# A batch's carry as an identity matmul into PSUM, one register load per batch, full-width clears

## The chip, the cores and the metric

One core of a Trainium2 chip. The time is device microseconds (us) of the whole program. The median of three runs of the kernel before is 1608.08 us (1603.89 to 1608.5).

## The reference

A three-layer graph step over 3125 nodes of 256 features with 50000 weighted edges (dst sorted, src not), and then a mixture of 16 experts, top 2. What matters here is the graph step, whose sparse matrix the kernel first builds as a dense one, for use in all three layers:

```
def _spmm(vals, row, col, h, n_nodes):
    msgs = vals[:, None] * h[col]
    return segment_sum(msgs, row, num_segments=n_nodes)
for _ in range(LAYERS):
    h = _l2_normalize(_spmm(vals, row, col, h, n_nodes));  acc = acc + h
x = x + acc / (LAYERS + 1)
```

In the program's call row is src and col is dst, and the edge list is sorted by dst. The output is x after that and after the expert layer.

## The kernel before

The program runs six phases one after another: phase_tables, phase_build, phase_rounds, phase_route, phase_experts, phase_combine. The change touches the first two; a barrier of all engines stands between phases.

phase_tables turns the sorted edge list into tables. Edges lie in tiles of 128. A step pairs one tile with one window of destination nodes (CW nodes, whose HI x LO rows of sources fill 120 x 160 numbers); tile and window advance like a staircase, so that there are 912 steps (STEPS), in 76 batches (NB) of 12 (B, BATCH). The tables hold for each step the marks of its edges (marks: key, low part of the source, the weight in three bf16 parts) and its place in PSUM (place: a slot of 160 columns, three slots to a bank of 512, four banks), and for each batch the window it starts at (base) and the slot of the batch before in which its first window lies (slot, by line 288). same says whether two batches share an edge tile's step at their border.

phase_build makes the dense matrix a_rows in DRAM. Per batch b:

- VectorE (one_hots, weigh, lines 465 to 480) compares tables with marks: key_hot (line 470), lo_hot (472), and three weighted copies key_w (479), the third only for half of the steps. It starts batch b when batch b - 2 is multiplied (two buffers, u).
- ScalarE (third, line 424) makes the other six third weights (433), and evacuates the four banks of PSUM into win, a ring of four batches (evacuate, 436, line 444).
- TensorE (multiply, 541) waits for the evacuation of batch b - 2, loads registers with the places of two batches in every even batch (24 registers, line 547), clears four banks with matmuls on zeros that are 2 columns wide (552, start=True), waits for hot_ready and third_ready, and adds 12 x 3 matmuls of 128 x 160 (558) at the places in the registers.
- VectorE adds the carry of batch b - 2 (carry, 496, line 504): the slot of the batch before it, in which a window was left unfinished, times same_b, onto its first slot in win. The slots are registers, four loaded per four batches (slots_of, 488, line 491); same_b is copied out by line 486.
- SP (store, 400) loads base (401), waits for carried, and stores the batch's window rows in four DMAs, one for each 32 partitions (406); each waits for the same part of the batch before.

Batches are unrolled at both ends and loop by four in between (batches, 383, and Fori at 522). phase_rounds reads a_rows after the barrier.

Of the kernel before, what the change touches and what calls it, by code (L numbers as in the profile page):

```python
# [21 lines left out]
I32 = mybir.dt.int32  # L22
U32 = mybir.dt.uint32
ALU = mybir.AluOpType
# [65 lines left out]
def phase_tables(nc, s, x, src, dst, ew, hf, tab):  # L90
    with ExitStack() as ctx:
# [124 lines left out]
        def _(dve):  # L216
# [41 lines left out]
            link(v.tensor_tensor(win_of[:], step_id[:], tile_of[:], ALU.subtract))  # L258
            first = tile_of[:].rearrange("p (b j) -> p b j", j=B)
            v.memset(tab.same[:, 0:1], 0.0)  # L260
            v.tensor_tensor(tab.same[:, 1:s.NB], first[:, 1:s.NB, 0], first[:, 0:s.NB - 1, B - 1], ALU.subtract)

# [24 lines left out]
            link(v.tensor_tensor(moved[:, 1:s.NB], base[:, 1:s.NB], base[:, 0:s.NB - 1], ALU.subtract))  # L287
            link(v.tensor_scalar(moved[:], moved[:], float(B - 1), float(s.LO), ALU.min, ALU.mult))
            v.tensor_copy(tab.slot[:], moved[:])
            v.tensor_scalar(tab.base[:], base, float(s.W - 1), None, ALU.min)  # L290
# [4 lines left out]
            link(v.scalar_tensor_tensor(bank[:], slot[:], float(s.LO), bank[:], ALU.mult, ALU.add))  # L295
            link(v.tensor_copy(tab.place[:], bank[:]))

# [33 lines left out]
def phase_build(nc, s, tab, a_dram):  # L331


    with ExitStack() as ctx:
# [16 lines left out]
        zeros = sb("zeros", [P, s.HI * LO])  # L351
        same_b = sb("same_b", [P, 2])
        third_b = sb("third_b", [P, 2, B])
        none = sb("none", [P, 512], BF16)
        win = sb("win", [P, RING, B * LO])
        ps_w = ctx.enter_context(nc.psum_tensor("ps_w", [P, 2, BANKS * 512], F32))

        tabs = sem("tabs")
        same_read = sem("same_read")
        third_read = sem("third_read")  # L360
# [4 lines left out]
        evacuated = sem("evacuated")  # L365
        carried = sem("carried")
        padded = sem("padded")
# [25 lines left out]
        @block.sync  # L393
        def _(sp):
            first = s.W * CW
            sp.wait_ge(tabs, 3)
            sp.dma_start(a_dram.rearrange("i (c n) l -> (i c) (n l)", c=CW)[first:s.CH * P, :],
                         zeros[0:s.CH * P - first, :]).then_inc(padded, 16)

            def store(b, i):  # L400
                base = sp.value_load(tab.base[0:1, one(b)], min_val=0, max_val=s.W - 1)
                sp.wait_ge(carried, b + 1)
                for n, part in enumerate(PARTS):
                    if late(b, 1):
                        sp.wait_ge(stored[n], b * 16)
                    sp.dma_start(a_dram[bass.DynSlice(base, B), part, :].rearrange("i p l -> p i l"),
                                 win[part, i, :].rearrange("p (i l) -> p i l", l=LO)).then_inc(stored[n], 16)

            sp.wait_ge(padded, 16)
            for b in range(NB):  # L410
                store(b, b % RING)
            for done in stored:
                sp.wait_ge(done, 16 * NB)

        @block.gpsimd
        def _(pool):
            g = nc.gpsimd
            g.memset(none[:], 0.0).then_inc(tabs, 1)
            g.memset(zeros[:], 0.0).then_inc(tabs, 1)
            g.memset(win[:, RING - 1, :], 0.0).then_inc(tabs, 1)  # L420

        @block.scalar
        def _(act):
# [12 lines left out]
            def evacuate(b, i):  # L436
                if late(b, RING):
                    act.wait_ge(carried, b - 2)
                    for done in stored:
                        act.wait_ge(done, (b - 3) * 16)  # L440
                act.wait_ge(tabs, 3)
                act.wait_ge(multiplied, b + 1)
                for bank in range(BANKS):
                    ins = nc.scalar.activation(win[:, i, bank * WIDE:(bank + 1) * WIDE],  # L444
                                               ps_w[:, i % 2, bank * 512:bank * 512 + WIDE], ACT.Copy)
                ins.then_inc(evacuated, 1)
# [10 lines left out]
        def _(dve):  # L457
# [23 lines left out]

            def same(b, u):

                if late(b, 2):
                    dve.wait_ge(carried, b - 1)
                v.tensor_copy(same_b[:, u:u + 1], tab.same[:, one(b)]).then_inc(same_read, 1)

            def slots_of(b, n):

                at = slice(b, b + n) if isinstance(b, int) else bass.DynSlice(b, n)  # L490
                _, values = nc.values_load_multi_w_load_instructions(
                    tab.slot[0:1, at], engines=[mybir.EngineType.DVE], min_val=0, max_val=(B - 1) * LO,
                    skip_runtime_bounds_check_because="a slot is LO times the minimum with B - 1 of a count")
                return values

            def carry(b, i, slot):

                there = bass.DynSlice(slot, LO)
                start = slice(0, LO)
                dve.wait_ge(evacuated, b + 1)  # L500
                dve.wait_ge(same_read, b + 1)
                if late(b, 1):
                    dve.wait_ge(carried, b)
                v.scalar_tensor_tensor(win[:, i, start], win[:, (i - 1) % RING, there], same_b[:, i % 2:i % 2 + 1],
                                       win[:, i, start], ALU.mult, ALU.add).then_inc(carried, 1)

            def run(b, i, slot):
                u = i % 2
                one_hots(b, u)
                weigh(b, u, 0)  # L510
                weigh(b, u, 1)
                if late(b, 2):
                    same(b - 2, u)
                weigh(b, u, 2)
                if late(b, 2):
                    carry(b - 2, (i - 2) % RING, slot)

            dve.wait_ge(tabs, 3)
            slots = slots_of(0, 2)
            for b in range(RING):  # L520
                run(b, b, slots[b - 2] if b >= 2 else None)
            with dve.Fori(1, NB // RING) as it:
                slots = slots_of(it * RING - 2, RING)
                for i in range(RING):
                    run(it * RING + i, i, slots[i])
            slots = slots_of(NB - 2, 2)
            for b in (NB - 2, NB - 1):
                same(b, b % 2)
                carry(b, b % RING, slots[b - (NB - 2)])

        @block.tensor
        def _(pe):
            mm = nc.tensor.matmul
            pe.wait_ge(tabs, 3)
            for bank in range(2 * BANKS):
                mm(ps_w[:, bank // BANKS, bank % BANKS * 512:(bank % BANKS + 1) * 512], none[:, 0:P], none[:, :],
                   start=True, stop=True, skip_group_check=True)

            places = []

            def multiply(b, i):
                u = i % 2
                if late(b, 2):
                    pe.wait_ge(evacuated, b - 1)
                if u == 0:
                    both = slice(b * B, (b + 2) * B) if isinstance(b, int) else bass.DynSlice(b * B, 2 * B)
                    places[:] = nc.values_load_multi_w_load_instructions(
                        tab.place[0:1, both], engines=[mybir.EngineType.PE], min_val=0,
                        max_val=(BANKS - 1) * 512 + (PER - 1) * LO,
                        skip_runtime_bounds_check_because="a place is made of a slot below B, whatever the edges are")[1]  # L550
                for bank in range(BANKS):
                    mm(ps_w[:, u, bank * 512:bank * 512 + 2], none[:, 0:P], none[:, 0:2],  # L552
                       start=True, stop=False, skip_group_check=True)
                pe.wait_ge(hot_ready, (b + 1) * 4)
                pe.wait_ge(third_ready, (b + 1) * BY_ACT)
                for j in range(B):
                    for k in range(3):
                        ins = mm(ps_w[:, u, bass.DynSlice(places[u * B + j], LO)], key_w[:, u, k, j // 2, :, j % 2],  # L558
                                 lo_hot[:, u, j // 2, :, j % 2],
                                 start=False, stop=False, skip_group_check=True)  # L560
                ins.then_inc(multiplied, 1)

# [1120 lines left out]
class Tables:  # L1683


    def __init__(self, nc, ctx, s):
# [5 lines left out]
        self.marks = sb("tab_marks", [P, 5, s.STEPS], BF16)  # L1692
        self.same = sb("tab_same", [P, s.NB])
        self.place = sb("tab_place", [1, s.STEPS], I32)
        self.slot = sb("tab_slot", [1, s.NB], I32)
        self.base = sb("tab_base", [1, s.NB], I32)
# [45 lines left out]
```

## Time and profile before

| | us |
|---|---|
| median of 3 runs | 1608.08 (1603.89 to 1608.5) |
| the profiled execution | 1605.87 |
| its span, first to last instruction | 1604.1 |

The page's first part gives for the whole span: TensorE busy 1259.8 us (79%), VectorE 1137.9 (71%), ScalarE 875.4 (55%), GpSimd 209.8 (13%), and a mean granted TensorE clock of 0.878, where 1 is 2.4 GHz and 0.5 is 1.2 GHz. phase_build runs from some 49 to 465 us. Busy time is that of compute instructions; what a sequencer does (register loads, waits) has rows of its own and isn't in it, and the engine's idle time that comes of it is put down to "issue". Names in rows: PE is TensorE, PEld its weight loads, PEldq and DVEq the sequencers of TensorE and VectorE, SPq SP's queue, DVE VectorE, ACT ScalarE, POOL GpSimd.

### The profile page before, as it was taken

The page shows a single profiled execution, that of the slowest core. Times are in us where ns is not written, and L with a number is a line of the kernel's source. Part 1 is how long each engine was busy: PE and PEld are TensorE (multiplying, and loading weights), DVE is VectorE, ACT ScalarE, POOL GpSimd, SP SyncE. Part 2 cuts the span into 40 slices and gives each one's busy share as a digit, 9 for nine tenths or more (in the row PEclk, how much of TensorE's full clock was granted, in tenths as well). Part 3 has the DMA queues.
Part 4 walks back from the last instruction along what each step waited for, and adds up shares of the span by engine and source line. Part 5 has one row for each costly group of instructions (what it writes and reads, how often), then busy time and mean ns, then how long its engine had stood idle before and what let it go on. Part 6 is the DMA issues. An engine that isn't in the chain of part 4 may idle for free. (4 is left out here: it accounts for less than half of the span.)

```text
span 1604.1 us, 31106 instructions
## 1 busy us (share of the span) xinstructions
PE 1259.8 (79%) x9152; PEld 1135.5 (71%) x9153; DVE 1137.9 (71%) x2074; ACT 875.4 (55%) x1933; POOL 209.8 (13%) x199
## 2 busy tenths in 40 slices
PE   4467666667648999999999999999754799999600
PEld 1366666666647888888888888888652699999600
DVE  8788888888837656656555766655567498898557
ACT  2577777777735555655545655555321466666312
POOL 1300000000000000000000000000080434444273
PEclk8788887888879999999999999999955799999955
DMA  3187777677787666656666666666222587334373
GB/s 95 45 206 189 181 178 173 166 173 174 182 235 209 183 187 185 182 166 178 187 194 183 187 166 186 176 195 183 88 95 70 188 269 235 109 103 110 118 232 113
DMA packets 228741, 267.64 MB, mean 167 GB/s; under 512 B 16053, under 2 KB 172348, under 8 KB 228582
## 3 DMA queue, kind: packets, MB, share of 16 engines
q1 hardware_dynamic: 205392, 234.01, 52.5%
q0 software_dynamic: 6624, 16.90, 3.9%
q10 hardware_dynamic: 16640, 15.73, 3.2%
q8 instruction: 36, 0.59, 0.1%
q14 instruction: 49, 0.40, 0.1%
HBM read 175.51 MB, written 91.07 MB: 166 GB/s over the span
## 5 line engine op out<-in xcount | busy, mean ns | idle before, releaser
L865 PE MATMUL ps_rows<-h_both,a_high 128*128 (+1 forms) x1875 | 509.7, 400 | 29.4 <-DVE a_low L745 24.1
L745 DVE TENSOR_TENSOR a_low<-a_raw,a_high 128x640 fp32r<-128x640 f32 x375 | 305.8, 823 | 239.0 <-ACT a_high L675 236.0
L675 ACT ACTIVATE a_high<-a_raw 128x640 fp32r<-128x640 f32 x375 | 274.6, 740 | 297.2 <-PE ps_rows L868 283.5
L865 PEld LDWEIGHTS ps_rows<-h_both,a_high 128*128 128x128 f32 x1875 | 332.7, 192 | 87.7 <-issue 24.5
L868 PEld LDWEIGHTS ps_rows<-h_both,a_low 128*128 128x128 f32 x1875 | 277.4, 191 | 33.2
L868 PE MATMUL ps_rows<-h_both,a_low 128*128 (+1 forms) x1875 | 285.7, 283 | 0.0
L558 PE MATMUL ps_w<-lo_hot,key_w 128*128 128x160 bf16 x2736 | 258.5, 264 | 33.1 <-DVE key_w L479 31.0
L558 PEld LDWEIGHTS ps_w<-lo_hot,key_w 128*128 128x128 bf16 x2736 | 243.4, 112 | 37.7 <-issue 35.9
L444 ACT ACTIVATE win<-ps_w 128x480 f32<-128x480 f32 x304 | 147.3, 567 | 71.5 <-PE ps_w L558 57.6
L479 DVE TENSOR_TENSOR key_w<-key_hot,tab_marks 128x1536 bf16<-128x1536 bf16 (+1 forms) x228 | 178.2, 814 | 0.0
L433 ACT ACTIVATE key_w<-key_hot,third_b 128x128 bf16<-128x128 bf16 x456 | 144.5, 426 | 38.2 <-DVE key_hot L470 36.9
L1353 POOL DMA_INDIRECT x_t<-tokens,r_token x80 | 104.4, 1305 | 131.5 <-PE ps_x L1480 118.7
L1367 ACT ACTIVATE w_high<-w_raw 128x1024 fp32r x80 | 80.4, 1052 | 63.1 <-PE ps_o L1512 53.6
L470 DVE TENSOR_TENSOR key_hot<-key_tab,tab_marks 128x1536 bf16<-128x1536 bf16 x76 | 72.3, 951 | 58.6 <-PE ps_w L558 31.2
L1425 DVE TENSOR_TENSOR w_low<-w_raw,w_high 128x1024 fp32r<-128x1024 f32 x80 | 94.4, 1220 | 17.6 <-ACT w_high L1367 12.9
L1495 PE MATMUL ps_h<-x_high,w_high 128*128 128x256 f32 x320 | 94.8, 296 | 0.0
L1011 POOL MEMSET all_ones<- 128x800 f32 x1 | 0.8, 764 | 699.5 <-POOLq L572 699.5
L1495 PE MATMUL ps_h<-x_low,w_high 128*128 128x256 f32 x320 | 91.4, 286 | 0.0
L1495 PE MATMUL ps_h<-x_high,w_low 128*128 128x256 f32 x320 | 91.4, 286 | 0.0
L1512 PE MATMUL ps_o<-w_high,hid_high 128*128 128x256 f32 x320 | 90.0, 281 | 1.3 <-DVE hid_low L1440 1.3
L552 PE MATMUL ps_w<-none 128*128 128x2 bf16 x304 | 18.9, 166 | 91.3 <-issue 91.3
L1512 PE MATMUL ps_o<-w_low,hid_high 128*128 128x256 f32 x320 | 90.1, 281 | 0.0
(225 smaller groups left out, 1576.0 us busy)
## 6 DMA issues: line engine op xcount, KB each, us to landing
a_raw<-a_rows SPq DMA_DIRECT2D x375, 320.0 KB, 3.1
a_rows<-win SPq DMA_DIRECT2D x228, 240.0 KB, 3.6
w_raw<-in_L_ffn_w SPq DMA_DIRECT2D x32, 512.0 KB, 5.0
a_rows<-win SPq DMA_DIRECT2D x76, 180.0 KB
results_sorted<-y_t ACTq DMA_DIRECT2D x40, 256.0 KB, 3.2
b_t<-in_L_ffn_b ACTq DMA_DIRECT2D x40, 128.0 KB, 3.6
hf<-in_x SPq DMA_DIRECT2D x1, 3072.0 KB
x<-in_x SPq DMA_DIRECT2D x1, 3072.0 KB
```

The lines of the kernel that those rows point to most:

```text
L433: nc.scalar.activation(key_w[:, u, 2, j // 2, :, j % 2], key_hot[:, u, j // 2, :, j % 2], ACT.Copy, scale=third_b[:, u, j:j + 1]).then_inc ...
L444: ins = nc.scalar.activation(win[:, i, bank * WIDE:(bank + 1) * WIDE], ps_w[:, i % 2, bank * 512:bank * 512 + WIDE], ACT.Copy)
L479: v.tensor_tensor(key_w[:, u, k, 0:n, :, :], key_hot[:, u, 0:n, :, :], mark(b, 2 + k, P)[:, 0:n, :, :], ALU.mult).then_inc(hot_ready, 1)
L558: ins = mm(ps_w[:, u, bass.DynSlice(places[u * B + j], LO)], key_w[:, u, k, j // 2, :, j % 2], lo_hot[:, u, j // 2, :, j % 2], start=False ...
L675: a.activation(a_high[:, u, :], a_raw[:, u, :], ACT.Copy).then_inc(high_split, 1)
L745: v.tensor_tensor(a_low[:, u, :], a_raw[:, u, :], a_high[:, u, :].bitcast(F32), ALU.subtract).then_inc(low_split, 1)
L865: nc.tensor.matmul(ps[:, banks[w][r], :], a_high[:, u, r * P:(r + 1) * P], both, start=first, stop=False, skip_group_check=True)
L868: ins = nc.tensor.matmul(ps[:, banks[w][r], 0:D], a_low[:, u, r * P:(r + 1) * P], upper, start=False, stop=last, skip_group_check=True)
L1353: g.indirect_dma_start(out=x_t[:, t % 2, h, :], out_offset=None, in_=y_dram, in_offset=bass.IndirectOffsetOnAxis(ap=routes.token[:, t * HA ...
L1425: v.tensor_tensor(w_low[n][:, u, :], of_expert(w_raw[n], e), w_high[n][:, u, :].bitcast(F32), ALU.subtract).then_inc(w_low_ready[n], 1)
L1495: ins = mm(ps_h[:, u, f, :], w[0][:, u, at], x[:, u, k, :], start=(n == 0), stop=(n == 3 * KD - 1))
L1512: ins = mm(ps_o[:, u, half, :], h[:, u, f, tokens], w[1][:, u, at], start=(n == 0), stop=(n == 3 * KF - 1))
```

## The change

The carry moves from VectorE to TensorE. After a batch's 36 matmuls TensorE waits for the evacuation of the batch before (evacuated, b) and multiplies the identity (fp32, made by GpSimd) with the 160 columns of win that hold the slot, into the batch's first place. same, same_b, the semaphores same_read and carried, and tab.slot are gone; whether there is a carry is now told by the slot alone: it is limited to B instead of B - 1, and win has a thirteenth slot of zeros. tab.place holds 13 numbers per batch, twelve places and the slot, and TensorE loads them in one load per batch, behind the clears. The clears are 512 columns wide, and the eight full clears at the start of the phase are gone. SP waits for evacuated. VectorE's loop has no register load. The waits on tabs move: VectorE and ScalarE have none, TensorE waits for 5.

```diff
-            link(v.tensor_scalar(moved[:], moved[:], float(B - 1), float(s.LO), ALU.min, ALU.mult))
-            v.tensor_copy(tab.slot[:], moved[:])
+            link(v.tensor_scalar(moved[:], moved[:], float(B), float(s.LO), ALU.min, ALU.mult))
+            v.tensor_copy(tab.place[:, :, B], moved[:])
...
-            link(v.tensor_copy(tab.place[:], bank[:]))
+            link(v.tensor_copy(tab.place[:, :, 0:B], bank[:].rearrange("p (b j) -> p b j", j=B)))
...
-        win = sb("win", [P, RING, B * LO])
+        win = sb("win", [P, RING, (B + 1) * LO])
...
-                sp.wait_ge(carried, b + 1)
+                sp.wait_ge(evacuated, b + 1)
...
-            g.memset(win[:, RING - 1, :], 0.0).then_inc(tabs, 1)
+            g.memset(win[:, :, B * LO:(B + 1) * LO], 0.0).then_inc(tabs, 1)
+            g.memset(ones[:], 1.0).then_inc(tabs, 1)
+            pool.wait_ge(tabs, 4)
+            g.affine_select(out=ident[:], in_=ones[:], pattern=[[1, P]], compare_op=ALU.is_equal,
+                            fill=0.0, base=0, channel_multiplier=-1).then_inc(tabs, 1)
...
                 if late(b, RING):
-                    act.wait_ge(carried, b - 2)
                     for done in stored:
                         act.wait_ge(done, (b - 3) * 16)
-                act.wait_ge(tabs, 3)
                 act.wait_ge(multiplied, b + 1)
...
-                v.scalar_tensor_tensor(win[:, i, start], win[:, (i - 1) % RING, there], same_b[:, i % 2:i % 2 + 1],
-                                       win[:, i, start], ALU.mult, ALU.add).then_inc(carried, 1)
...
+            def run(b, i):
                 u = i % 2
                 one_hots(b, u)
...
+                for k in range(3):
+                    weigh(b, u, k)
+
+            batches(dve, run)
...
-            pe.wait_ge(tabs, 3)
-            for bank in range(2 * BANKS):
-                mm(ps_w[:, bank // BANKS, bank % BANKS * 512:(bank % BANKS + 1) * 512], none[:, 0:P], none[:, :],
-                   start=True, stop=True, skip_group_check=True)
...
+            pe.wait_ge(tabs, 5)
...
                 if late(b, 2):
                     pe.wait_ge(evacuated, b - 1)
-                if u == 0:
-                    both = slice(b * B, (b + 2) * B) if isinstance(b, int) else bass.DynSlice(b * B, 2 * B)
-                    places[:] = nc.values_load_multi_w_load_instructions(
-                        tab.place[0:1, both], engines=[mybir.EngineType.PE], min_val=0,
...
                 for bank in range(BANKS):
-                    mm(ps_w[:, u, bank * 512:bank * 512 + 2], none[:, 0:P], none[:, 0:2],
+                    mm(ps_w[:, u, bank * 512:(bank + 1) * 512], none[:, 0:P], none[:, :],
                        start=True, stop=False, skip_group_check=True)
+                values = nc.values_load_multi_w_load_instructions(
+                    tab.place[0:1, one(b), :].rearrange("p b j -> p (b j)"), engines=[mybir.EngineType.PE], min_val=0,
+                    max_val=B * LO,
...
                 pe.wait_ge(hot_ready, (b + 1) * 4)
                 pe.wait_ge(third_ready, (b + 1) * BY_ACT)
...
+                if late(b, 1):
+                    pe.wait_ge(evacuated, b)
+                    ins = mm(ps_w[:, u, bass.DynSlice(places[0], LO)], ident[:, :],
+                             win[:, (i - 1) % RING, bass.DynSlice(slot, LO)],
+                             start=False, stop=False, skip_group_check=True)
                 ins.then_inc(multiplied, 1)
...
-        self.place = sb("tab_place", [1, s.STEPS], I32)
-        self.slot = sb("tab_slot", [1, s.NB], I32)
+        self.place = sb("tab_place", [1, s.NB, s.BATCH + 1], I32)
```

## Rows read from the trace of the kernel before

**Rows 1.** Windows view, all engines: us, busy and count, clock, DMA share, GB/s

```profile
60.00:465.00 405.00, 268.18 (x3031) 257.04 (x3028) 339.47 (x527) 291.98 (x828) 0.00 (x0) 0.83 0.73 175
```

**Rows 2.** Groups by line, 80 to 440: busy us, mean ns, then idle before

```profile
L479 DVE TENSOR_TENSOR key_w<-key_hot,tab_marks 128x1536 bf16<-128x1536 bf16 (+1 forms) x207 | 161.9, 814 | 0.0
L444 ACT ACTIVATE win<-ps_w 128x480 f32<-128x480 f32 x276 | 133.7, 566 | 68.3 <-PE ps_w L558 55.4 <-DMA a_rows<-win 12.9
L433 ACT ACTIVATE key_w<-key_hot,third_b 128x128 bf16<-128x128 bf16 x413 | 131.0, 426 | 25.8 <-DVE key_hot L470 24.6
```

**Rows 3.** Waits, 80 to 440: who waited for what, us in total, times, longest

```profile
PE ps_w L552 <- issue: 88.3, 34, 4.2
DVE key_hot L470 <- issue: 17.3, 7, 3.1
```

**Rows 4.** Single lines, several stretches: count, ns min/median/max, first and last start

```profile
L547 PEldq TENSOR_LOAD <-tab_place x2: 1622/1627/1632, 65.1 to 73.8; - x2
...
L491 DVEq TENSOR_LOAD <-tab_slot x1: 986/986/986, 72.1 to 72.1; - x1
...
L547 PEldq TENSOR_LOAD <-tab_place x34: 1952/3346/4654, 84.1 to 431.8; - x34
...
L491 DVEq TENSOR_LOAD <-tab_slot x17: 1700/2315/3541, 91.5 to 427.6; - x17
...
L547 PEldq TENSOR_LOAD <-tab_place x1: 3797/3797/3797, 293.9 to 293.9; - x1
...
L558 PEldq FUSED_REGOPS  x9: 37/37/42, 297.9 to 298.9; - x9
```

**Rows 5.** Timeline of TensorE: start us, us, what, [idle before <- released by]

```profile
291.98 2.75 PE L558 MATMUL ps_w<-lo_hot,key_w 128*128 128x160 bf16 x36 [0.25 <-DVE key_w L479]
297.72 0.25 PE L552 MATMUL ps_w<-none 128*128 128x2 bf16 x4 [2.99 <-issue]
298.03 4.02 PE L558 MATMUL ps_w<-lo_hot,key_w 128*128 128x160 bf16 x36
...
308.70 4.98 PE L558 MATMUL ps_w<-lo_hot,key_w 128*128 128x160 bf16 x36 [0.91 <-DVE key_w L479]
```

**Rows 6.** Timeline of VectorE around one batch

```profile
291.13 0.14 DVE L486 COPY same_b<-tab_same 128x1 f32 x1
291.19 0.55 DVE L479 TENSOR_TENSOR key_w<-key_hot,tab_marks 128x768 bf16<-128x768 bf16 x1
291.65 0.38 DVE L504 SCALAR_TENSOR_TENSOR win<-win,same_b 128x160 f32<-128x160 f32 x1
291.95 0.95 DVE L470 TENSOR_TENSOR key_hot<-key_tab,tab_marks 128x1536 bf16<-128x1536 bf16 x1
...
296.45 0.95 DVE L470 TENSOR_TENSOR key_hot<-key_tab,tab_marks 128x1536 bf16<-128x1536 bf16 x1
```

**Rows 7.** Timeline at the phase's two ends

```profile
54.27 3.60 PE L536 MATMUL ps_w<-none 128*128 128x512 bf16 x8 [16.32 <-POOL win L420]
...
55.08 0.96 DVE L470 TENSOR_TENSOR key_hot<-key_tab,tab_marks 128x1536 bf16<-128x1536 bf16 x1 [9.13 <-POOL win L420]
...
59.45 2.75 PE L558 MATMUL ps_w<-lo_hot,key_w 128*128 128x160 bf16 x36 [1.50 <-DVE key_w L479]
...
448.39 2.74 PE L558 MATMUL ps_w<-lo_hot,key_w 128*128 128x160 bf16 x36
...
465.27 2.27 SPq L643 DMA_DIRECT2D a_raw<-a_rows  x5
```

**Rows 8.** SP: its register load (78 to 138, then all), and the page's DMA issues

```profile
L401 SPq TENSOR_LOAD <-tab_base x14: 479/692/1094, 78.5 to 137.4; - x14
...
L401 SPq TENSOR_LOAD <-tab_base x76: 467/728/1170, 74.3 to 456.8; - x76
...
a_rows<-win SPq DMA_DIRECT2D x228, 240.0 KB, 3.6
```

**Rows 9.** Single line 1182, a matmul in full fp32 of the route phase

```profile
L1182 PEld LDWEIGHTS ps_l<-gw,yT x100: 287/333/337, 1180.6 to 1209.5; 128*128 128x128 f32 x100
```

More of the change, by code:

```diff
@@ L258, in _ @@
             link(v.tensor_tensor(win_of[:], step_id[:], tile_of[:], ALU.subtract))
-            first = tile_of[:].rearrange("p (b j) -> p b j", j=B)
-            v.memset(tab.same[:, 0:1], 0.0)
-            v.tensor_tensor(tab.same[:, 1:s.NB], first[:, 1:s.NB, 0], first[:, 0:s.NB - 1, B - 1], ALU.subtract)
             dve.wait_ge(x_in, 32)
@@ L351, in phase_build @@
         zeros = sb("zeros", [P, s.HI * LO])
-        same_b = sb("same_b", [P, 2])
+        ones = sb("ones_c", [P, P])
+        ident = sb("ident_c", [P, P])
         third_b = sb("third_b", [P, 2, B])
         none = sb("none", [P, 512], BF16)
-        win = sb("win", [P, RING, B * LO])
+        win = sb("win", [P, RING, (B + 1) * LO])
         ps_w = ctx.enter_context(nc.psum_tensor("ps_w", [P, 2, BANKS * 512], F32))
         tabs = sem("tabs")
-        same_read = sem("same_read")
         third_read = sem("third_read")
@@ L365, in phase_build @@
         evacuated = sem("evacuated")
-        carried = sem("carried")
         padded = sem("padded")
@@ L406, in store @@
                     sp.dma_start(a_dram[bass.DynSlice(base, B), part, :].rearrange("i p l -> p i l"),
-                                 win[part, i, :].rearrange("p (i l) -> p i l", l=LO)).then_inc(stored[n], 16)
+                                 win[part, i, 0:B * LO].rearrange("p (i l) -> p i l", l=LO)).then_inc(stored[n], 16)
             sp.wait_ge(padded, 16)
@@ L480, in weigh @@
                                 ALU.mult).then_inc(hot_ready, 1)
[L482 to L503, printed above, removed]
-                v.scalar_tensor_tensor(win[:, i, start], win[:, (i - 1) % RING, there], same_b[:, i % 2:i % 2 + 1],
-                                       win[:, i, start], ALU.mult, ALU.add).then_inc(carried, 1)
-            def run(b, i, slot):
+            def run(b, i):
                 u = i % 2
                 one_hots(b, u)
[L510 to L529, printed above, removed]
+                for k in range(3):
+                    weigh(b, u, k)
+            batches(dve, run)
         @block.tensor
@@ L533, in _ @@
             mm = nc.tensor.matmul
-            pe.wait_ge(tabs, 3)
-            for bank in range(2 * BANKS):
-                mm(ps_w[:, bank // BANKS, bank % BANKS * 512:(bank % BANKS + 1) * 512], none[:, 0:P], none[:, :],
-                   start=True, stop=True, skip_group_check=True)
-            places = []
+            pe.wait_ge(tabs, 5)
             def multiply(b, i):
@@ L544, in multiply @@
                     pe.wait_ge(evacuated, b - 1)
-                if u == 0:
-                    both = slice(b * B, (b + 2) * B) if isinstance(b, int) else bass.DynSlice(b * B, 2 * B)
-                    places[:] = nc.values_load_multi_w_load_instructions(
-                        tab.place[0:1, both], engines=[mybir.EngineType.PE], min_val=0,
-                        max_val=(BANKS - 1) * 512 + (PER - 1) * LO,
-                        skip_runtime_bounds_check_because="a place is made of a slot below B, whatever the edges are")[1]
                 for bank in range(BANKS):
-                    mm(ps_w[:, u, bank * 512:bank * 512 + 2], none[:, 0:P], none[:, 0:2],
+                    mm(ps_w[:, u, bank * 512:(bank + 1) * 512], none[:, 0:P], none[:, :],
                        start=True, stop=False, skip_group_check=True)
+                values = nc.values_load_multi_w_load_instructions(
+                    tab.place[0:1, one(b), :].rearrange("p b j -> p (b j)"), engines=[mybir.EngineType.PE], min_val=0,
+                    max_val=B * LO,
+                    skip_runtime_bounds_check_because="a place is made of a slot up to B, whatever the edges are")[1]
+                places, slot = [nc.s_assert_within(
+                    place, min_val=0, max_val=(BANKS - 1) * 512 + (PER - 1) * LO,
+                    skip_runtime_bounds_check_because="it is the place of a slot below B") for place in values[0:B]], values[B]
                 pe.wait_ge(hot_ready, (b + 1) * 4)
@@ L557, in multiply @@
                     for k in range(3):
-                        ins = mm(ps_w[:, u, bass.DynSlice(places[u * B + j], LO)], key_w[:, u, k, j // 2, :, j % 2],
+                        ins = mm(ps_w[:, u, bass.DynSlice(places[j], LO)], key_w[:, u, k, j // 2, :, j % 2],
                                  lo_hot[:, u, j // 2, :, j % 2],
                                  start=False, stop=False, skip_group_check=True)
+                if late(b, 1):
[3 more added lines that the diff above has]
+                             start=False, stop=False, skip_group_check=True)
                 ins.then_inc(multiplied, 1)
@@ L1692, in __init__ @@
         self.marks = sb("tab_marks", [P, 5, s.STEPS], BF16)
-        self.same = sb("tab_same", [P, s.NB])
-        self.place = sb("tab_place", [1, s.STEPS], I32)
-        self.slot = sb("tab_slot", [1, s.NB], I32)
+        self.place = sb("tab_place", [1, s.NB, s.BATCH + 1], I32)
         self.base = sb("tab_base", [1, s.NB], I32)
```

## The prediction

> **What bounds the kernel now.** I read the windows first, to find the stage of the change: from 60 to 465 us no engine is full, VectorE is busy 339 us of 405, TensorE 268, ScalarE 292, the DMA engines 0.73, and TensorE's mean granted clock is 0.83 [rows 1]. From 465 us on nothing of the change runs. Then the table of groups in the steady part, where the reader is to see what one batch costs each engine [rows 2]: of VectorE 2.35 us (three weights, 161.9 us for 69 batches), to which key_hot, lo_hot, same_b and the carry come; of ScalarE six weights that run overlapped (131.0 / 69 = 1.90) and the evacuation (133.7 / 69 = 1.94); of TensorE 36 matmuls, whose timeline gives 2.75 us at the full clock and 4.98 at the half [rows 5]. Third, the waits [rows 3]: the longest is TensorE before its four clears, 88.3 us, put down to "issue", so to no other engine; VectorE also waits 17.3 us for "issue". Fourth, the sequencers' rows, which are not counted as busy, name these two: a TENSOR_LOAD, which fetches registers from a table in SBUF [rows 4]. TensorE runs one of 24 registers every second batch (median 3.35 us in 80 to 440), VectorE one of 4 every fourth (2.32). The timeline shows what that does: a load begins at 293.9, beside the last matmuls of the batch that ran from 291.98 to 294.73, lasts 3.80, and the clears start at 297.72, after 2.99 us of idle engine [rows 4, 5].
>
> So two chains take turns. VectorE: 4.50 us from key_hot to key_hot (291.95 to 296.45 [rows 6]); four of them and a load of 2.3 give 20.3 per four batches. TensorE: its loads run from 84.1 to 431.8, 33 steps for 33 pairs [rows 4], 10.54 a pair, 5.27 a batch. Over the stage the first matmul is at 59.45 and the last batch's at 448.39 [rows 5, 7]: 388.9 / 75 = 5.19 us a batch.
>
> **Part 1: the carry leaves VectorE.** 0.38 + 0.14 busy; the next key_hot starts 0.30 after the carry does and the weight 0.06 after same_b [rows 6], so the path loses 0.36: 4.50 becomes 4.14. The load of 4 registers goes too (a median of 2.3 us). VectorE then needs 4 x 4.14 = 16.6 per four batches where it needed 20.3. This is worth 0.9 us a batch if VectorE were alone. It is not: TensorE and the stores are late next.
>
> **Part 2: TensorE's register load, the largest term.** Before: 38 loads of 24. After: 76 loads of 13, one in every batch, on the queue that all matmuls pass. Its time isn't in the trace, so it is bounded by its neighbours [rows 4]. While no store runs: 4 registers 0.99, 24 registers 1.63, which gives 1.28 for 13 on a line. While stores run: 4 take 2.32, 24 take 3.35 (up to 4.65). The ratios are 2.3 and 2.1, so the cost is mostly the company of the stores: line 406 has a store in flight 3.6 us after each issue [rows 8]. In the new order the load falls wholly into a store (below), where the load at 293.9 took 3.80, so I take 13 registers at 3.0, between 2.3 (as 4) and 3.8 (as 24).
>
> In sentences apart: the Trainium skill ("Runtime: NRT & Kernel Launch", Instruction fetch mechanics) says that such a load costs about 200 ns a register even in bulk. The rows don't agree, 4 registers taking 2.32 and 24 taking 3.35; by that rule 13 would be an estimated 2.6, the batch 4.8 and the time some 1571.
>
> **TensorE's cycle after.** Its sequencer runs ahead of the array: nine register steps of three matmuls each were issued from 297.9 to 298.9 [rows 4], 0.12 apart, while the array at the half clock took 0.13 per matmul. From a batch's first matmul: 12 x 0.12 = 1.4 to issue all 36; then the carry (its place and slot arithmetic), four clears and the address of the next load, all issue work, 0.45 (an estimate: the 0.33 between a load's end at 297.70 and the first matmul at 298.03 holds four clears and the steps of the waits [rows 4, 5], and a loop's branch comes every fourth time); the load 3.0; and 0.35 to the next first matmul. Sum 5.2 us a batch. The wait on evacuated in front of the carry stands ahead of the next clears and load on the same queue, so it could delay both. It is satisfied in time: the array ends batch b-1 (2.75, clears and carry behind it) 1.65 before batch b's first matmul, the evacuation takes 1.96 + 0.1 and ends 0.4 after it, and the sequencer reaches the wait at 1.5. ScalarE needs 1.90 + 1.94 and a small copy, 4.1 a batch [rows 2], in the same order as before, and VectorE 4.14: both fit in 5.2.
>
> **Part 3: clears over 512 columns and the carry on the array.** Array time, not issue time. A 512-column matmul on zeros starts each 0.43 us at the half clock (8 in 3.60 [rows 7]), so 0.21 at the full one, x4 = 0.85 where 0.24 stood. The carry is a matmul in full fp32: the rows of line 1182 [rows 9] show 100 entries where 50 were written, so two passes, 0.33 us per weight load at the half clock; for 160 columns I take 0.8 in all, bounds 0.3 and 1.3. At the full clock the array holds 2.6 + 0.85 + 0.8 = 4.2 of 5.2, and 1.0 idle lies inside the 3.0 load. So both are hidden by the load; without that cover they would cost 1.4 a batch. Nor should the clock fall: before, it was at the half level after idle of 2.8 to 3.0 us (the batch at 298.03, 4.02 long, follows a gap of 2.99 [rows 5]), and after no gap is over 1.3. I expect 1.0 in the stage, which gives no time back, since issue and load set the cycle.
>
> **Part 4: stores.** SP waits for evacuated instead of carried. A store could go one to two batches sooner, which frees the ring of win earlier; no time on the path. SP's pace is a floor: while it caught up, 14 of its loads ran from 78.5 to 137.4, 13 steps, 4.53 us a batch [rows 8].
>
> **Part 5: the edges.** POOL's memset of win shrinks to a third and ones and ident are added: I take it that tabs is complete at 54.1, about as before (TensorE started at 54.27 [rows 7]). VectorE no longer waits for it (9.13 us of idle before 55.08 [rows 7]) and is ready; TensorE drops the eight full clears (3.6), and its first matmul waits for a load, 54.1 + 2.7 + 0.4 = 57.2, where it was 59.45: -2.2. Batches 0 to 4, with loads of 1.3, run at VectorE's 4.15, 16.6 in all, the other 71 at 5.2: 385.8 instead of 388.9: -3.1; the stores start only at 74.3 [rows 8], a us sooner perhaps since POOL ends sooner, and the ring holds four batches, which gives back some 1.2. At the end the carries of the last two batches and the stores behind them leave 16.9 us from the last batch's first matmul to the next stage at 465.27 [rows 7]; after: 3.5 (array) + 2.1 + 2.3 (four stores issued) + 4.2 (landing) + 0.8 = 12.9: -4.0. The steps that VectorE loses in the tables stage are worth nothing: it stood idle for 9.13 before 55.08.
>
> **Sum.** -2.2 - 3.1 + 1.2 - 4.0 = -8.1 us: span 1604.1 to 1596.0. The profiled execution is 1605.87, 1.8 above its span and 2.2 below the median of 1608.08. I forecast 1600.0 against the median, -0.5%.
>
> **Rivals.**
> 1. The load is short, and the stores bound. If 13 registers cost 2.3 or less, TensorE's cycle is 4.5 and SP's 4.53 rules: 73.3 + 76 x 4.53 + 4.2 (the last landing) = 422 instead of 465.3, 43 us less, 1565. For it: 4 registers took down to 1.70 beside stores, 24 down to 1.95 [rows 4]. Against: the median of the 4 is already 2.32. The floor holds however short the load is. What lies between this case and mine, a load of 2.3 to 2.75 (1567 to 1582), goes with it. The Trainium skill's rule per register (same page and section) ends there.
> 2. The load costs nearly what 24 cost, since it is paid in every batch now. Place: TensorE's queue between the clears and the first matmul; price: 3.5 to 3.8 gives a cycle of 5.7 to 6.0, 71 x 0.5 - 8 = +28 to 71 x 0.8 - 8 = +49, 1636 to 1657. It decides from a load of 3.11, where the time is that of before. For it: 3.35 is the median of 24 with part of them outside the stores, and the twofold number of loads; against: 24 and 4 differ by 1.0 only, so 13 must lie between.
> 3. The array becomes the bound at the half clock: 4.98 + 1.7 (clears) + 0.9 = 7.6 a batch, +170, some 1778. It needs a clock that stays low; against it, an array that is behind has no gaps.
> 4. The change removes VectorE's work but both chains shift alike and the time stays within 0.3%; this is the middle of my own case.
>
> **How the numbers follow.** 0.3% (4.8 us) is about what a measurement of this kernel can tell. One tenth of a us in the cycle is 7 us. My case, a load of 2.75 to 3.25, has 0.46: 1582 to 1618 by itself, faster 0.26, same 0.13, slower 0.07. Rival 1 and what lies towards it: 0.20, all faster. Rival 2: 0.28, slower. Rival 3: 0.05, slower; rival 4 as a case by itself 0.01. So faster 0.46, same 0.14, slower 0.40. The range goes from rival 1's floor to the middle of rival 2 and leaves out rival 3: 1563 to 1642.
>
> **What would show it.** TensorE's TENSOR_LOAD x76 with a median near 3.0 between 80 and 440 (right), 2.3 (rival 1) or 3.5 (rival 2); first matmuls 5.2 apart; the granted clock near 1.0 in the stage (a 0.83 would break part 3); VectorE idle before key_hot in every batch, waiting for TensorE; no wait of the carry for the evacuation. I am wrong if the load waits for the array to drain, which the load at 293.9 didn't (matmuls until 294.73), or if the carry's wait comes late.

## The result, and the profile after

The changed kernel takes 1843.84 us (median of 4 runs, 1839.07 to 1844.89), the kernel before 1608.29 beside it: ratio 1.1466, 95% interval 1.1437 to 1.1495, slower by 235 us. The forecast was 1600.0, slightly faster, with a range of 1563 to 1642: the time is far above the range and above every rival, the slowest of which was 1778.

The profiled execution has a span of 1841.2 us, 237 more than before. Nearly all of it, 232.5, lies ahead of the next stage's start (697.73 where it was 465.27); the stages behind, which the change doesn't touch, are 4.6 longer. The windows of its steady part, after (first) and before (second); columns as in [rows 1]:

```profile
110.00:400.00 290.00, 173.91 (x1438) 148.93 (x1436) 144.51 (x173) 134.02 (x378) 0.00 (x0) 0.78 0.48 112
```

```profile
110.00:400.00 290.00, 199.07 (x2227) 191.09 (x2228) 248.74 (x386) 212.46 (x606) 0.00 (x0) 0.82 0.74 177
```

Every engine does less in the same 290 us, and the DMA engines move 112 GB/s where they moved 177: the pipeline waits for one thing. The stage's two ends, in TensorE's and SP's timeline, answer [rows 7]:

```profile
56.13 4.25 PE L511 MATMUL ps_w<-lo_hot,key_w 128*128 128x160 bf16 x36 [0.56 <-ACT key_w L433]
...
684.10 4.29 PE L511 MATMUL ps_w<-lo_hot,key_w 128*128 128x160 bf16 x36 [6.14 <-issue]
...
697.73 2.27 SPq L601 DMA_DIRECT2D a_raw<-a_rows  x5
```

(684.10 - 56.13) / 75 = 8.37 us a batch, where it was 5.19; 75 x 3.19 = 239, the whole loss. The waits, 80 to 640, answer [rows 3]:

```profile
ACT win L442 <- PE ps_w L516: 301.6, 49, 9.5
DVE key_hot L468 <- PE ps_w L516: 284.3, 36, 9.2
PE ps_w L511 <- issue: 221.9, 46, 7.3
```

VectorE waits for TensorE at 36 places and ScalarE at 49, of some 67 batches in this window. TensorE waits for its own sequencer and, but for 1.9 us, for nothing else; the wait now stands in front of the matmuls (line 511), since the clears go ahead of the load. The loads, one line each, all 76 and then five in a row, answer [rows 4]:

```profile
L500 PEldq TENSOR_LOAD <-tab_place x76: 1100/3310/8982, 53.7 to 675.8; - x76
...
L500 PEldq TENSOR_LOAD <-tab_place x1: 8871/8871/8871, 266.9 to 266.9; - x1
...
L500 PEldq TENSOR_LOAD <-tab_place x1: 1100/1100/1100, 279.4 to 279.4; - x1
...
L500 PEldq TENSOR_LOAD <-tab_place x1: 8094/8094/8094, 284.1 to 284.1; - x1
...
L500 PEldq TENSOR_LOAD <-tab_place x1: 3099/3099/3099, 295.9 to 295.9; - x1
...
L500 PEldq TENSOR_LOAD <-tab_place x1: 8738/8738/8738, 301.2 to 301.2; - x1
```

The same instruction with the same 13 registers takes 1.10, 3.10 or about 8 to 9 us, and the mean of all 76 is 5.16, where I had taken 3.0. The pattern repeats every four batches: 1.1, 8, 3.1, 8. A row of 13 words is 52 bytes, so batch b starts at 52 b, which lies on a 16-byte border for every fourth b.

The timeline of TensorE over two batches, to be read against [rows 5]:

```profile
282.27 2.74 PE L511 MATMUL ps_w<-lo_hot,key_w 128*128 128x160 bf16 x36
284.85 0.47 PE L516 MATMUL ps_w<-win,ident_c 128*128 x2
285.16 1.03 PE L498 MATMUL ps_w<-none 128*128 128x512 bf16 x4
292.56 4.98 PE L511 MATMUL ps_w<-lo_hot,key_w 128*128 128x160 bf16 x36 [6.38 <-issue]
297.34 0.82 PE L516 MATMUL ps_w<-win,ident_c 128*128 x2
297.95 1.23 PE L498 MATMUL ps_w<-none 128*128 128x512 bf16 x4
```

The load that begins at 284.1, 1.8 after the batch's first matmul, ends at 292.2, and the next first matmul is at 292.56: 1.8 + 8.1 + 0.4 = 10.3 is the step from this batch to the next. After 6.38 us of idle the array is at the half clock (4.98 for the 36).

### The profile page after: what moved, and what is told of

It is laid out like the page before. It is cut to its first block and busy times, and to the rows that moved or that the text cites. A ratio compares the mean times of both kernels' runs of the same rounds, so it can differ in the third digit from the quotient of the medians.

```text
span 1841.2 us, 30942 instructions
## 1 busy us (share of the span) xinstructions
PE 1371.9 (75%) x9294; PEld 1203.7 (65%) x9295; DVE 1114.0 (61%) x1920; ACT 879.0 (48%) x1933; POOL 212.1 (12%) x201
## 5 line engine op out<-in xcount | busy, mean ns | idle before, releaser
L511 PE MATMUL ps_w<-lo_hot,key_w 128*128 128x160 bf16 x2736 | 288.6, 281 | 250.7 <-issue 242.1
L511 PEld LDWEIGHTS ps_w<-lo_hot,key_w 128*128 128x128 bf16 x2736 | 271.1, 119 | 284.1 <-issue 280.4
L477 DVE TENSOR_TENSOR key_w<-key_hot,tab_marks 128x1536 bf16<-128x1536 bf16 (+1 forms) x228 | 174.1, 820 | 0.0
L498 PE MATMUL ps_w<-none 128*128 128x512 bf16 x304 | 81.0, 390 | 15.9 <-POOL ident_c L419 15.9
L1470 PE MATMUL ps_o<-w_high,hid_low 128*128 128x256 f32 x320 | 89.9, 281 | 0.0
```

The lines of the kernel that those rows point to most:

```text
L477: v.tensor_tensor(key_w[:, u, k, 0:n, :, :], key_hot[:, u, 0:n, :, :], mark(b, 2 + k, P)[:, 0:n, :, :], ALU.mult).then_inc(hot_ready, 1)
L511: ins = mm(ps_w[:, u, bass.DynSlice(places[j], LO)], key_w[:, u, k, j // 2, :, j % 2], lo_hot[:, u, j // 2, :, j % 2], start=False, stop=F ...
L1470: ins = mm(ps_o[:, u, half, :], h[:, u, f, tokens], w[1][:, u, at], start=(n == 0), stop=(n == 3 * KF - 1))
```

## The experiments

Three theories were formed from those rows. Theory A: a load whose first word lies on a 16-byte border fetches four registers at a time, any other one; each fetch costs some 0.25 us in quiet and over twice that beside a store. Theory B: only the number of loads and the stores beside them matter. Theory C: the fault is a row that crosses a 64-byte border.

**1. The rows padded to 16 words (e1).**

```diff
-        self.place = sb("tab_place", [1, s.NB, s.BATCH + 1], I32)
+        self.place = sb("tab_place", [1, s.NB, 16], I32)
```

with the load of words 0 to 12 of a row.

> The changed kernel with one edit: a batch's 13 registers start every 16 words of the table instead of every 13. Theory A (start address): a load whose first word lies on a 16-byte border fetches four registers at a time, any other one at a time; each fetch is about 0.25 us in quiet and 0.6 beside a store. Every load is then 4 fetches: 1.1 quiet, at most 2.4, where the changed kernel has a mean of 5.2. Cycle 4.5 to 4.7 us a batch (the stores' pace), time 1560 to 1580, ratio to before 0.97 to 0.98. Theory B (company and count): the 8 us loads are slow because there are 76 of them beside stores, wherever the words lie; nothing changes, 1840. Theory C (64-byte border): a row of 52 bytes crosses one in most batches; padded it doesn't, so as A.

Measured: 1600.34 us, ratio to the kernel before beside it 0.9856, interval 0.9819 to 0.9894: 1.4% faster than before and far from the changed kernel, from one number in a table's shape. Loads, windows, and the last batch's first matmul:

```profile
L500 PEldq TENSOR_LOAD <-tab_place x76: 1103/2718/3640, 53.6 to 426.4; - x76
```

```profile
110.00:400.00 290.00, 226.59 (x2409) 183.47 (x2436) 246.38 (x292) 230.74 (x642) 0.00 (x0) 1.00 0.82 191
```

```profile
429.79 2.75 PE L511 MATMUL ps_w<-lo_hot,key_w 128*128 128x160 bf16 x36 [1.24 <-issue]
```

B falls. The gain is smaller than A's numbers had it: beside stores four fetches take 2.72 in the median, not 2.4 at most, and the cycle is 4.98, not 4.5 to 4.7. The same kernel once more, on another chip, beside experiments 9 and 10:

> The padded kernel once more, on the chip of the two others: ratio 0.982 to 0.989, cycle 5.0. Against the kernel before with quads it should be slower by 0.3 us a batch, 20 us, if the identity matmul costs what its removal gave (0.35 us a batch).

Measured: ratio 0.9825, interval 0.9734 to 0.9916, cycle 5.03. The interval is wide because one run took 1566.47 us where two others took 1589.5 and 1589.7; that run has no trace, and why it was shorter stays open.

**2 and 3. The padded rows, the words starting one and two words in (e2, e3).**

```diff
-                    tab.place[0:1, one(b), 0:0 + B + 1].rearrange("p b j -> p (b j)"), ...
+                    tab.place[0:1, one(b), 1:1 + B + 1].rearrange("p b j -> p (b j)"), ...
```

This is e2 against e1, and the words are written one further, too; e3 has 2 in place of 1.

> As the padded table, but the 13 words start one word into each row of 16: no row crosses a 64-byte border, none starts on a 16-byte one. Theory A: 13 fetches in every batch, 3.1 us in quiet and 8.2 beside stores, cycle about 8.9, time 1860 to 1900. Theory B: 1840. Theory C: as the padded table without the shift, 1560 to 1580.

> The 13 words start two words into each row of 16, on an 8-byte border. Theory A as said (only 16-byte borders count): as the shift by one, 3.1 quiet, 8.2 beside stores, 1860 to 1900. If 8 bytes are fetched at a time where they can be: 7 fetches, 1.8 quiet and 4.3, cycle 6.0 to 6.5, time 1650 to 1700. Theory B: 1840. Theory C: 1560 to 1580.

Measured: 1869.53 and 1875.23 us (one run each), within A's 1860 to 1900. Loads of e2, then e3:

```profile
L500 PEldq TENSOR_LOAD <-tab_place x76: 3097/4325/8680, 53.6 to 691.8; - x76
```

```profile
L500 PEldq TENSOR_LOAD <-tab_place x76: 3097/4435/8980, 53.7 to 690.5; - x76
```

No load is under 3.1 any more, and 3.1 and some 8 alternate. A had counted 8.2 for every load and a cycle of 8.9; the cycles are 8.49 and 8.53, so A's kind is borne out and its price per batch was too high. C falls, since no row of e2 crosses a 64-byte border. An 8-byte border helps nothing: e3 is as e2.

**4. The kernel before, its table moved by one word (e4).** The places are written one word later and read there:

```diff
-                    both = ... bass.DynSlice(b * B, 2 * B)
+                    both = ... bass.DynSlice(b * B + 1, 2 * B)
```

> The kernel before with one edit: its table of places starts one word later, so that its loads of 24 leave the 16-byte border. Theory A: 24 fetches instead of 6, 6 us in quiet, 10 to 15 beside stores, where the kernel before has a mean of 3.2; 38 loads, so 38 x 7 to 38 x 11 us more: 1870 to 2030. Theories B and C: nearly no change, 1605 to 1620 (C: one border more in some loads).

Measured: 1868.33 us (one run), at the lower end of A's 1870 to 2030; B and C had nearly no change. None of the other parts of the change is in it, and it is 246 us slower than the kernel before on this chip (1622.46), where the change cost 235. Its loads, 10.2 us in the mean where they were 3.2:

```profile
L547 PEldq TENSOR_LOAD <-tab_place x38: 6839/10350/14166, 54.3 to 685.2; - x38
```

**5. The changed kernel with small stores (e5).** Each store moves one window instead of twelve, and a_rows is filled with zeros behind the last batch (not shown in the cut), so the output is not the reference's and only the build stage is read.

```diff
-                    sp.dma_start(a_dram[bass.DynSlice(base, B), part, :].rearrange("i p l -> p i l"),
-                                 win[part, i, 0:B * LO].rearrange("p (i l) -> p i l", l=LO)).then_inc(stored[n], 16)
+                    sp.dma_start(a_dram[bass.DynSlice(base, 1), part, :].rearrange("i p l -> p i l"),
+                                 win[part, i, 0:LO].rearrange("p (i l) -> p i l", l=LO)).then_inc(stored[n], 16)
```

> The changed kernel, its table as it is, but each store of a batch moves one of its twelve windows, a twelfth of the bytes; behind the last batch the whole of a_rows is filled with zeros in 25 transfers of 1.6 MB (some 215 us of their own), so the output isn't the reference's and the time of the whole says nothing. What is read is the build stage. Theory A (start address times company): loads of every fourth batch 1.1 us, all others 3.1, none of 8; mean 2.6; cycle 4.9 to 5.0, the last batch's first matmul at 425 to 435 instead of 684. If the company of the stores has no part in it: the 8 us loads stay, 684.

Measured: the last batch's first matmul at 427.66, so a cycle of 4.95, with the DMA engines 0.07 busy from 110 to 400, and nine loads in a row:

```profile
L504 PEldq TENSOR_LOAD <-tab_place x9: 1101/3103/3111, 197.0 to 236.6; - x9
```

The 8 us loads are gone, the 3.1 us ones stay. The two causes are so told apart: where the row starts gives 1.1 or 3.1, the stores make 8 of 3.1. The record of all 76 shows the two classes: loads of every fourth batch 1.16 in the mean, all others 3.1.

**6. The padded kernel with narrow clears (e6).** The clears of a batch are 2 columns wide and the eight full clears stand at the start of the stage, as in the kernel before.

> The padded table, but the four clears of a batch are 2 columns wide again, with the eight full ones at the start of the stage (a slot that no matmul wrote then keeps old numbers, which the carry may read). If the wide clears are hidden by the load, as the prediction had it, and the clock stays: the same time as the padded kernel within 0.3%. If the wide clears are what keeps the clock at its full level: granted clock of the stage 0.85 to 0.95 instead of 1.0, cycle 5.1 to 5.3, 8 to 25 us more. If the array counts after all: 10 to 20 us less.

Measured: ratio 0.9976, interval 0.9949 to 1.0004, on another chip than e1.

```profile
110.00:400.00 290.00, 195.85 (x2310) 188.98 (x2310) 231.86 (x276) 217.30 (x607) 0.00 (x0) 0.91 0.77 180
```

The granted clock is 0.91 where it is 1.00 in e1, the cycle 5.21 where it is 4.98 and, in e11, 5.03 ((447.68 - 56.91) / 75, from the first matmuls' starts). The loads are the same (median 2.72 both). So the wide clears are worth having here: they cost array time that the load hides, and with them the array doesn't fall to the half clock in the steady batches. The prediction had counted them as hidden, but not as a gain.

**7. One load for two batches (e7).** The padded table by pairs, 28 registers in every second batch.

> The padded table laid out by pairs of batches (24 places, 2 slots, the slots once more), one load of 28 registers every second batch: 7 fetches of four for two batches where the padded kernel has 8 in two loads. By issue and load alone the cycle is (2 x 2.1 + 4.2) / 2 = 4.2, so the stores' pace of 4.53 sets the end: last batch's first matmul at 395 to 405, 20 to 33 us less than the padded kernel, ratio to before 0.965 to 0.975. Rival: the gap of 2 us in every second batch lets the clock fall, and the slower array gives the gain back: ratio 0.98 to 0.99, clock under 0.95.

Measured: ratio 1.0243, interval 1.0169 to 1.0317: slower than before, where the padded kernel is faster. I had the loads right and the rest wrong.

```profile
L505 PEldq TENSOR_LOAD <-tab_place x38: 1877/4359/5646, 53.6 to 470.4; - x38
...
L505 PEldq TENSOR_LOAD <-tab_place x1: 4592/4592/4592, 256.3 to 256.3; - x1
```

The waits (80 to 380) seem to name ScalarE's weights; the timeline shows that it isn't they:

```profile
PE ps_w L516 <- ACT key_w L435: 69.7, 24, 3.5
```

```profile
254.11 2.74 PE L516 MATMUL ps_w<-lo_hot,key_w 128*128 128x160 bf16 x36
...
255.62 1.90 ACT L435 ACTIVATE key_w<-key_hot,third_b 128x128 bf16<-128x128 bf16 x6
...
259.43 1.90 ACT L435 ACTIVATE key_w<-key_hot,third_b 128x128 bf16<-128x128 bf16 x6
...
261.21 4.17 PE L516 MATMUL ps_w<-lo_hot,key_w 128*128 128x160 bf16 x36 [3.18 <-ACT key_w L435]
```

The matmuls at 261.21 use the weights that were done at 257.5; those of 259.43 are for the batch behind. The load ends at 260.9, and 0.35 later the matmuls start, as in the padded kernel. So the load is what the array waits for. In 29 steady pairs the weights of ScalarE are done 2.9 us or more before a pair's first matmul, VectorE's 2.4 or more, and the first matmul follows the load's end by 0.26 to 0.35 in all of them. The expectation had counted 2.1 of issue for each of the two batches. But the second batch starts only when the array has done the first: 3.76 us later at the full clock, 5.35 at the half (means). Then come 2.0 of issue, 4.4 of load and 0.35. That is 10.5 us a pair at the full clock, where the padded kernel takes twice 4.98, and 12.0 at the half; 14 of the 29 pairs are of the second kind, such as the one at 261.21, behind 3.18 us of idle. One load for two batches saves about 1.1 us of load time a pair, but no load runs beside the first batch's array time any more.

**8. The padded kernel without the carry's matmul (e8).**

> The padded table; the identity matmul of the carry is left out (the wait in front of it stays), so a window that spans two batches loses the part of the first. If the carry costs array time alone it is hidden by the load: issue 0.1 to 0.2 us less a batch, 5 to 15 us in all. If its end is what starts the next chain (the evacuation, then VectorE and ScalarE) and this chain binds: 0.6 to 0.8 us a batch, 40 to 60 us.

Measured: 1564.07 us against 1604.53 of the kernel before (one run): the last first matmul at 403.50, a cycle of 4.63. By the profiled executions the carry costs 0.35 a batch, 26 us, between the two guesses. This isn't settled: it is one run, the padded kernel's ratios put it at 1576 to 1581 on this chip, only 12 to 17 us more, and one run of e11 took 1566.47 with the carry in it. Of the 0.35, 0.14 is issue (the load begins 1.86 after the first matmul with it, 1.72 without), and 0.22 is in the load itself (mean 2.61 and 2.39), for which I have no shown cause; that the load then falls at another time beside the store is only argued. The stage is now at the stores' pace, 4.53 [rows 8]: over the steady batches the cycle is 4.53, and each batch's store is issued 7.6 us behind its evacuation in the mean and doesn't catch up, where in e1 that lag falls to 0.2.

**9 and 10. Two versions of the kernel before, with the carry on VectorE (e9, e10).** e9 moves the table of slots by two words, so that VectorE's load of four starts on a border; e10 has that and, in every batch, wide clears and behind them one load of 12:

```diff
+                places = nc.values_load_multi_w_load_instructions(
+                    tab.place[0:1, steps(b)], engines=[mybir.EngineType.PE], ...
```

> The kernel before with one edit: the table of slots starts two words later, so that VectorE's load of four begins on a 16-byte border. Theory A: one fetch instead of four, 0.3 us in quiet, 0.6 beside stores, where it has a mean of 2.3; VectorE's four batches take 18.6 us instead of 20.3. TensorE's chain of 10.5 us a pair stands beside it, so the gain is at most half of 1.7 per four batches: 0 to 16 us, ratio 0.990 to 1.0. If start addresses didn't matter: load 2.3, ratio 1.0.

> The kernel before (carry on VectorE) with VectorE's slots on the border, one load of 12 registers in every batch (rows of 48 bytes, all on 16-byte borders, 3 fetches) behind clears of 512 columns; no full clears at the start. So two thirds of the change, without the carry's matmul. Theory A: loads 0.85 quiet, 1.8 beside stores; TensorE's cycle 4.1, VectorE's 4.5 + 0.6/4 = 4.65 binds, clock near 1.0; last batch's first matmul at 59 + 75 x 4.7 = 411, ratio 0.975 to 0.985. If a load in every batch is itself the fault: slower than before.

Measured: e9 0.9915 (0.9885 to 0.9944), e10 0.9793 (0.9762 to 0.9825), 1571.8 us, the lowest ratio of the kernels that were run several times. Their loads, VectorE's of e9 and TensorE's of e10:

```profile
L491 DVEq TENSOR_LOAD <-tab_slot x20: 345/902/997, 54.3 to 433.7; - x20
```

```profile
L542 PEldq TENSOR_LOAD <-tab_place x76: 850/2225/2793, 54.3 to 413.3; - x76
```

The first has a median of 0.90 where it was 2.32 [rows 4], and in quiet, at 72.1, it took 0.38 where it was 0.99. This is VectorE's load, so the start address and not the engine made it dear. The second shows that a load in every batch is no fault: twice the loads of before, and faster. e10 has a cycle of 4.76 ((416.07 - 59.44) / 75) and waits for VectorE's weights (57.3 us of TensorE's waits from 80 to 380). So in the traces the carry is cheaper on VectorE (4.76 against 4.98 to 5.03), though VectorE is then the bound; the intervals of e10 and e11 overlap, and the times alone don't decide it.

## Why the prediction was wrong

The step that failed is one term of part 2, the load of 13 registers: 3.0 predicted, 5.16 measured in the mean. Two things were wrong in it.

- "which gives 1.28 for 13 on a line": I drew a line through a load of 4 (0.99) and one of 24 (1.63) as if both were of one kind. They aren't: the 24 start at a multiple of 96 bytes, on a 16-byte border, and are 6 fetches; the 4 start 8 bytes beside one and are 4 fetches. What I took for a fixed cost with 0.03 a register is some 0.25 a fetch. The rows hinted at it, 0.25 us a register for the one and 0.07 for the other, and with the stores 0.58 and 0.14; I read the difference as curvature. The rows alone didn't prove it, for the two loads also ran on different engines; e9 sets that aside. Counted in fetches, the same four rows give the padded load 1.1 in quiet and 2.2 to 2.3 beside stores (2.7 measured) and the unpadded one 3.2 and 7.3 to 7.5 (3.1 and some 8 measured).
- Both bounds, "2.3 (as 4) and 3.8 (as 24)", rested on the number of registers, so no rival came near the measured load. The nearest rows were near in count and far in where they start.

The Trainium skill ("Runtime: NRT & Kernel Launch", Instruction fetch mechanics) gives about 200 ns a register for a TENSOR_LOAD, with the register loads that the runtime puts in as its case; the table here is the kernel's own and lies in SBUF. I set the figure aside because the 24 disagreed. It is near what the runs show for loads off the border in quiet, 3.10 / 13 = 0.24. For loads on it they show 1.62 / 6 = 0.27 for four.

Point by point, the rest:

- The cycle, issue + load + 0.35: right where the batch runs at the full clock. There the load begins 1.85 after the first matmul (1.85 predicted) and the next first matmul is 0.36 after its end; 1.85 + 8.38 + 0.36 = 10.6 us is the mean step with a long load, and the padded kernel's 4.98 is 1.86 + 2.7 + 0.36 with some branches. What was missing: where the array is at the half clock, the load begins 3.3 after the first matmul instead of 1.85. Half the batches of the changed kernel are such. And behind a load of 1.1 in such a batch the next first matmul comes 1.74 after the load's end, for the array isn't done yet. Over 59 steady batches the step is 8.48 in the mean; of the 3.3 us above 5.2, 2.2 are the loads, 0.7 the later start of the load and 0.4 the wait behind the short loads.
- The stores more than double a load's time: right (3.1 to 8, 1.1 to 2.7), and e5 shows it by taking them away.
- Part 1, VectorE's gain goes into a wait for TensorE: right, 284 us of wait from 80 to 640, most of it from the longer cycle (the padded kernel has 50.8 from 80 to 400).
- Part 3, clears and carry hidden by the load: right for the array's time, where the load is the bound. The clock at 1.0: right in the padded kernel, wrong in the changed one (0.78), because its gaps are 6 to 7 us and not 1.3. That the wide clears hold the clock up (e6) was not in it.
- The carry's matmul: 0.8 of array time and no cost predicted; at the full clock its two passes took 0.47, and the clears start 0.31 after it (284.85 and 285.16 above). A cost of 0.35 a batch, as the one run of e8 has it, wasn't foreseen.
- Part 4, the stores' pace as a floor of 4.53: right, e8 stands on it in its steady batches.
- Part 5: first matmul at 56.13 (57.2 predicted), 13.6 us from the last first matmul to the next stage (12.9 predicted). Right.
- The rivals: rival 2, in which a load costs what 24 registers cost because it stands in every batch, is out by e10 (2.2 for 12 in every batch). Rival 1, the stores' pace as the bound, is reached by e8 alone. Rival 3, the half clock as the bound, came in no kernel as a steady state: in the changed one the half clock follows from the long loads, and only one batch in four is held by the array. (Its 1778 also leaves out the 8 us that the other sums take off; 1770 by the same sum.)

## What to carry to other kernels

The times of the register loads here follow a count of fetches: start each row of a table on a 16-byte border, padding it if needed, before anything is done about how many registers or loads there are. Before a cost is drawn between two rows, see that the two agree in everything that the new case has (here the start address and the engine), not only in the size on the axis. Before two loads are joined to save a part of one, see what array time runs beside each of them: a load in every batch had some of it, and the joined one had that of one batch in two. And when a wait names a producer, check in the timeline that it made what this instruction reads.

## What the runs showed of the hardware

TENSOR_LOAD while no store runs, the least of each kind (borders are counted from the table's start):

| registers | start | fetches | us | kernel |
|---|---|---|---|---|
| 4 (VectorE) | 16-byte border | 1 | 0.38 | e9 |
| 4 (VectorE) | 8 bytes beside it | 4 | 0.99 | before |
| 12 | border | 3 | 0.85 | e10 |
| 13 | border | 4 | 1.10 | after, e1 |
| 13 | 4, 8 or 12 bytes beside it | 13 | 3.10 | after, e2, e3, e5 |
| 24 | border | 6 | 1.62 | before |
| 28 | border | 7 | 1.88 | e7 |

That is 0.24 to 0.28 a fetch in all but the first row. Beside stores that keep the DMA engines 0.74 to 0.82 busy a fetch takes 0.56 (24 registers, median 3.35) to 0.74 (12 registers, median 2.22). The count of fetches is inferred from these times; no run shows the fetches themselves. Whether it is the memory's port or the path to it that the stores fill was not tried.
